# Expert outputs scattered with an add onto normalised rows in DRAM, instead of two stored rows per token

## The reference

```python
x = x + gnn(layernorm(x), edges, ...)
h = layernorm(x)                                    # "normalised rows"
# for every row: the 2 best of 16 experts, softmax weights w0, w1 over the two logits
moe = w0 * expert_e0(h) + w1 * expert_e1(h)         # expert: relu(h @ w1 + b1) @ w2 + b2, 256 -> 512 -> 256
y = h + moe
out = x + layernorm(y) * gamma + beta
```

## Time and profile before

| | |
|---|---|
| median of 3 runs | 1053.31 us (1049.52 to 1053.36) |
| the profiled execution | 1059.64 us |
| its span | 1057.8 us |
| engine busy in the span | PE 698.1, DVE 687.2, POOL 456.7, ACT 417.3 us |
| mean granted TensorE clock | 0.82 of 2.4 GHz |
| DMA | 178.11 MB, 168 GB/s over the span |

### The profile page before, as it was taken

One profiled execution on the slowest core, in us unless ns is written; L12 is line 12 of the kernel. 1 busy time (PEld: TensorE's weight loads), 2 busy tenths in 40 slices (PEclk: granted clock), 3 DMA queues, 4 the chain that ended last, 5 costly groups with the idle time before them and its releaser, 6 DMA issues. The chain is left out here.

```text
span 1057.8 us, 21646 instructions
## 1 busy us (share of the span) xinstructions
PE 698.1 (66%) x6132; PEld 609.6 (58%) x6132; DVE 687.2 (65%) x1486; ACT 417.3 (39%) x1089; POOL 456.7 (43%) x655
## 2 busy tenths in 40 slices
PE   3666878887515334230499999999999999970000
PEld 3553655555204333230399999999999999960000
DVE  7998999999269988812145555555444444435984
ACT  5933777776112222220133333333334333321331
POOL 9200000000002888845057777777555555540422
PEclk9997899999655555555599999999999999995555
DMA  9906756752171342224677766767676676625672
GB/s 290 247 7 49 191 160 159 174 173 52 57 237 51 116 143 98 84 74 141 242 210 216 211 212 212 214 211 212 213 214 211 212 211 213 211 81 174 243 240 70
DMA packets 100597, 178.11 MB, mean 168 GB/s; under 512 B 25247, under 2 KB 69153, under 8 KB 97055
## 3 DMA queue, kind: packets, MB, share of 16 engines
q1 hardware_dynamic: 75092, 145.28, 45.8%
q0 software_dynamic: 10512, 27.88, 7.5%
q10 hardware_dynamic: 14880, 3.60, 2.8%
HBM read 139.53 MB, written 37.20 MB: 167 GB/s over the span
## 5 line engine op out<-in xcount | busy, mean ns | idle before, releaser
L1133 PEld LDWEIGHTS PS<-W 128*128 128x128 f32 x1808 | 221.8, 193 | 8.7 <-issue 2.1
L1133 PE MATMUL PS<-W 128*128 128x128 f32 x1808 | 222.6, 277 | 2.2 <-DMA W<-in_L_ffn_w 1.7
L1144 PE MATMUL PS<-W 128*128 x904 | 213.7, 379 | 0.0
L1144 PEld LDWEIGHTS PS<-W 128*128 128x128 f32 x904 | 164.1, 191 | 17.5
L1291 POOL DMA_INDIRECT ys<-W x113 | 121.6, 1076 | 115.5 <-DVE W L1249 88.2
L691 DVE TENSOR_TENSOR W<-R,W 128x3584 bf16<-128x3584 bf16 (+1 forms) x104 | 159.4, 1590 | 0.0
L859 POOL DMA_INDIRECT xs<-W,slot_i x98 | 120.9, 1234 | 88.2 <-DVE slot_i L1008 59.9
L1221 DVE TENSOR_SCALAR W<-PS,b1T 128x128 f32<-128x128 f32 x226 | 70.2, 347 | 115.3 <-PE PS L1133 84.5
L1174 ACT ACTIVATE W<-PS 128x256 f32<-128x256 f32 x113 | 43.3, 383 | 257.3 <-PE PS L1121 155.2
L544 ACT ACTIVATE W<-PS 112x1024 f16<-112x1024 f32 x104 | 105.7, 1020 | 40.1 <-PE PS L603 38.7
L863 POOL MEMSET R<- 128x261 f32 x1 | 0.3, 317 | 254.3 <-POOLq L360 254.3
(11 more groups left out here) (215 smaller groups left out, 1154.5 us busy)
## 6 DMA issues: line engine op xcount, KB each, us to landing
W<-in_L_ffn_w SPq DMA_DIRECT2D x129, 512.0 KB, 8.8
W<-key_rows SPq DMA_DIRECT2D x26, 896.0 KB
W<-xs SPq DMA_DIRECT2D x113, 130.5 KB
W<-ys SPq DMA_DIRECT2D x6, 1792.0 KB, 8.1
XH<-in_x SPq DMA_DIRECT2D x6, 896.0 KB, 11.2
W<-in_x SPq DMA_DIRECT2D x7, 768.0 KB
out<-W SPq DMA_DIRECT2D x6, 896.0 KB, 4.1
W<-in_L_ffn_b ACTq DMA_DIRECT2D x1, 2048.0 KB, 7.5
```

The lines of the kernel that those rows point to most:

```text
L1133: last = nc.tensor.matmul(PS[:, 2 + 2 * u + j // 2, (j % 2) * P:(j % 2 + 1) * P], W1S[:, b, k, j * P:(j + 1) * P], XT3[:, u, k, :], start= ...
L1144: last = nc.tensor.matmul(PS[:, 6 + u, 0:C], HT3[:, u, j, :], wt2(e * W2COLS, j), start=(j == 0), stop=(j == 3))
```

## The change

`ys` now has one row per token, and behind them the rows for padding slots. The routing stage writes the normalised rows of each group there. The expert stage's scatters carry `compute_op=ALU.add`: the DMA reads the destination row, adds, and writes it back. Since two experts' tiles may meet in one row, `send(t)` waits until the scatter of tile t − 1 has landed. With the normalised row already in DRAM, ACT's `keep`, its buffer `Z1` and its semaphore go, `base_of` has one tensor input instead of two, and SP's reload of `X3[b]` waits for POOL's and ACT's small reads of that buffer in place of `keep`. The last stage reads one row per token (896 KB a group), DVE has no sum of two rows, and the residual is added by DVE where POOL did it.

```diff
-TRASH = 2 * NT * P
+TRASH = NT * P
...
+                def keep_rows(g, u, last):
+                    sp.wait_ge(xn_ready, GT * (g + 1))
+                    head = (GT - 1) * P
+                    sp.dma_start(ys[ds(g * (GT * P), head), :].rearrange("(t p) c -> p t c", p=P),
+                                 xn[:, u, 0:GT - 1, 0:C]).then_inc(xn_kept[u], 16)
+                    rows = LAST if last else P
+                    sp.dma_start(ys[ds(g * (GT * P) + head, rows), :], xn[0:rows, u, GT - 1, 0:C]).then_inc(xn_kept[u], 16)
+
+                def load_and_keep(g, i, u, last):
+                    load_x(g, i, u, last)
+                    if not (isinstance(g, int) and g == 0):
+                        keep_rows(g - 1, 1 - u, False)
+                pairs(sp, load_and_keep)
+                keep_rows(NGT - 1, 0, True)
...
                     wait_past(act, xn_sent[u], (16 * 2 * GT) * i)
+                    wait_past(act, xn_kept[u], 32 * i)
...
-                        sp.wait_ge(kept_ready, t + 1)
+                        sp.wait_ge(ratio_ready, t + 1)
+                        sp.wait_ge(first_ready, t + 1)
...
-                def keep(t):
-                    b = t % XBUFS
-                    act.wait_ge(first_ready, t + 1)
-                    if t >= 2:
-                        act.wait_ge(base_ready, t - 1)
-                    act.activation(Z1[:, t % 2, :], X3[:, b, 0:C], ACT.Copy, scale=first[:, b:b + 1]).then_inc(kept_ready, 1)
...
-                    nc.vector.scalar_tensor_tensor(Z3[:, t % 2, :], b2_bc[:, ds(e, 1), :].rearrange("p o c -> p (o c)"),
-                                                   weight[:, b:b + 1], Z1[:, t % 2, :], ALU.mult, ALU.add).then_inc(base_ready, 1)
+                    nc.vector.tensor_scalar(Z3[:, t % 2, :], b2_bc[:, ds(e, 1), :].rearrange("p o c -> p (o c)"),
+                                            weight[:, b:b + 1], None, ALU.mult).then_inc(base_ready, 1)
...
                 def send(t):
                     b, o = t % XBUFS, t % OBUFS
                     pool.wait_ge(o_ready, t + 1)
+                    if t >= 1:
+                        pool.wait_ge(o_sent[(t - 1) % OBUFS], 16 * ((t - 1) // OBUFS + 1))
                     nc.gpsimd.indirect_dma_start(
                         out=ys[:, :], out_offset=bass.IndirectOffsetOnAxis(ap=home[:, b:b + 1], axis=0),
-                        in_=O3[:, o, :], in_offset=None).then_inc(o_sent[o], 16)
+                        in_=O3[:, o, :], in_offset=None, compute_op=ALU.add).then_inc(o_sent[o], 16)
...
-                    y = y_two[u]
-                    nc.vector.tensor_tensor(y[:, :, 0, :], y[:, :, 0, :], y[:, :, 1, :], ALU.add).then_inc(y_summed, 1)
-                    dve.wait_ge(y_summed, g + 1)
                     for j in range(GT):
-                        ins = nc.vector.bn_stats(st4[:, j, :], y[:, j, 0, :])
+                        ins = nc.vector.bn_stats(st4[:, j, :], y_two[u][:, j, :])
...
+                    dve.wait_ge(scaled_ready, g + 1)
+                    nc.vector.tensor_tensor(scaled[u], scaled[u], XH[:, g * GT:(g + 1) * GT, :], ALU.add
+                                            ).then_inc(out_ready, 1)
...
-            @block.gpsimd
-            def _(pool):
-                for g in range(NGT):
-                    u = g % 2
-                    pool.wait_ge(scaled_ready, g + 1)
-                    nc.gpsimd.tensor_tensor(scaled[u], scaled[u], XH[:, g * GT:(g + 1) * GT, :], ALU.add
-                                            ).then_inc(out_ready, 1)
```

More of the change, by code:

```diff
@@ L180, in build @@
         O3 = take([OBUFS, C], fp32)
-        Z1 = take([2, C], fp32)
         Z3 = take([2, C], fp32)
@@ L193, in build @@
         take, at = carve(W, 0)
-        y_two = [take([GT, 2, C], fp32) for _ in range(2)]
+        y_two = [take([GT, C], fp32) for _ in range(2)]
         y_hat = [take([GT, C], fp32) for _ in range(2)]
@@ L386, in _ @@
                 const(pool.memset(cnt_in[:, :, :], 0.0))
-                const(pool.iota(tokc[:, :], pattern=[[2 * P, NT]], base=1, channel_multiplier=2,
+                const(pool.iota(tokc[:, :], pattern=[[P, NT]], base=0, channel_multiplier=1,
                                 allow_small_or_imprecise_dtypes=True))
@@ L807, in build @@
         token_set = sem("token_set")
+        xn_kept = [sem("xn_kept0"), sem("xn_kept1")]
         logits_sent = sem("logits_sent")
@@ L837, in load_x @@
                                  ).then_inc(xin_in[u], 16)
-                pairs(sp, load_x)
+                def keep_rows(g, u, last):
[11 more added lines that the diff above has]
+                keep_rows(NGT - 1, 0, True)
                 sp.wait_ge(pads_ready, 1)
@@ L849, in _ @@
                 sp.wait_ge(pads_in, 16 * (E + 1))
+                for u in range(2):
+                    sp.wait_ge(xn_kept[u], 32 * (NGT - NGT // 2 if u == 0 else NGT // 2))
             @block.gpsimd
@@ L1075, in build @@
         home_ready = sem("home_ready")
-        kept_ready = sem("kept_ready")
         base_ready = sem("base_ready")
@@ L1210, in _ @@
                         ratio_of(t + 1)
-                    keep(t)
             @block.vector
@@ L1274, in prepare @@
                     pool.wait_ge(first_ready, t + 1)
-                    nc.gpsimd.tensor_scalar(home[:, b:b + 1], X3[:, b, C + 4:C + 5], first[:, b:b + 1], trash[:, t:t + 1],
-                                            ALU.subtract, ALU.min
+                    nc.gpsimd.tensor_scalar(home[:, b:b + 1], X3[:, b, C + 4:C + 5], trash[:, t:t + 1], None, ALU.min
                                             ).then_inc(home_ready, 1)
@@ L1304, in build @@
         y_in = [sem("y_in0"), sem("y_in1")]
-        y_summed = sem("y_summed")
         st4_ready = sem("st4_ready")
@@ L1323, in load @@
                         sp.wait_ge(hat_ready, GT * (g - 1))
-                    sp.dma_start(y_two[u][:, 0:full].rearrange("p t k c -> p t (k c)"),
-                                 ys[2 * g * GT * P:2 * (g * GT + full) * P, :].rearrange("(t p k) c -> p t (k c)", p=P, k=2)
+                    sp.dma_start(y_two[u][:, 0:full], ys[g * GT * P:(g * GT + full) * P, :].rearrange("(t p) c -> p t c", p=P)
                                  ).then_inc(y_in[u], 16)
                     if g == NGT - 1:
-                        sp.dma_start(y_two[u][0:LAST, GT - 1].rearrange("p k c -> p (k c)"),
-                                     ys[2 * (NT - 1) * P:2 * N, :].rearrange("(p k) c -> p (k c)", k=2)
-                                     ).then_inc(y_in[u], 16)
+                        sp.dma_start(y_two[u][0:LAST, GT - 1], ys[(NT - 1) * P:N, :]).then_inc(y_in[u], 16)
                 def store(g):
@@ L1403, in hat @@
                     for j in range(GT):
-                        act.activation(y_hat[u][:, j, :], y_two[u][:, j, 0, :], ACT.Identity, bias=nm4[:, u, j:j + 1],
+                        act.activation(y_hat[u][:, j, :], y_two[u][:, j, :], ACT.Identity, bias=nm4[:, u, j:j + 1],
                                        scale=rs4[:, u, j:j + 1]).then_inc(hat_ready, 1)
```

1 line of the change is left out of this document (removed).

## The result

The changed kernel takes 1173.14 us (median of 4 runs, 1170.18 to 1174.14) against 1053.3 before: ratio 1.1155 (the two medians alone give 1.114), interval 1.1121 to 1.119, so 11 to 12% slower. The profiled execution took 1172.89 us, its span 1171.1.

What follows compares the result with a forecast made beforehand. PE was taken to bound the expert stage and a ring through POOL's addition the last stage. Last stage −28.2, expert loop 0, its end +2.8 and routing 0 sum to −25.4 us: 1053.31 to 1027.9, range 1022 to 1112.

Steps and rivals of the forecast that it cites:

- the scatters become the pace: Expert-stage rival: landings above 3.4 us lengthen the loop; 1120 us at a 4.2 us landing; chance 0.35.
- I take 3.2 us, and the loop costs 0: Expert stage: an accumulating scatter lands after 3.2 us, so waiting for it adds nothing to the 3.75 us tile.
- I take 0.35 with the semaphore: Expert stage: POOL needs 0.35 us from a scatter's landing to the next start, from 0.30 between back-to-back scatters.
- the limit for the landing: Expert stage: an accumulating scatter may take 3.4 us to land before the loop lengthens beyond 3.75 us.
- the bounds of 2.6 and 4.6: Accumulating scatter's landing: 2.6 us if the destination read hides entirely, 4.6 with a complete DRAM read ahead of the write.
- A plain scatter that waits for its predecessor would have a period of 2.95: Expert stage: a plain landing of 2.6 us plus 0.35 to the next start, against the tile's 3.75.
- Last stage, −28.2: Last stage: 28.2 us saved from 101.15, between −22 with slow loads and −31; groups 8.2 us apart.
- the two paths of the prediction: Last stage: ring through ACT at 8.2 us per group, or 7 us loads pacing two groups in 18.4 us.
- POOL's list has 0.2 us to spare with `beta`: Expert stage: POOL's own work plus 0.35 takes 3.55 us of 3.75 in the 49 tiles with `beta`.
- small overrun: Expert-stage rival: landing of 3.4 to 3.6 us or longer descriptors give back 5 to 22 us; chance 0.10.
- End of the stage, +2.8: End of the expert stage: the last scatter waits 3.55 us instead of 1.38 and lands 0.6 later, adding 2.8 us.
- Routing stage, 0: Routing stage: 14 added stores cost 0, with 0 to +13 us if ACT's cover were gone.

Runs made afterwards that it cites:

- b_wait: Kernel before, plain scatters, with only the wait for the previous scatter added: 1152.14 us, ratio 1.0843.
- b_wait_light: Kernel before plus the wait, plain scatters, half the first weights' bytes loaded from tile 4 on: 1103.04 us, ratio 1.0384.
- b_wait_noload: Kernel before plus the wait, plain scatters, no first weights loaded after tile 3: 1063.38 us, ratio 1.0024.
- t_nowait: Changed kernel with two rows per token, accumulating scatters without the wait, last stage reading one of the rows: 1043.47 us, ratio 0.9813.
- t_wait2: Changed kernel with two rows per token, accumulating scatters waiting for the one two tiles ago, last stage reading one row: 1046.51 us, ratio 0.9838.

## Why the prediction was wrong

The forecast was 1027.9 us, faster; measured is 1173.1, and outside the range. The side had been the first rival, "the scatters become the pace", with 0.35, and its case went further than its price of 1120. What failed is the step "I take 3.2 us, and the loop costs 0": the waiting scatters had a loop of 3.2 + 0.35 = 3.55 us in the sum, under PE's 3.75, and the runs show 5.07. Three things make up the difference of 1.5 us.

- **"I take 0.35 with the semaphore", from landing to the next start: 0.43 too little.** It is 0.78. The 0.30 came from a scatter that followed another on POOL. The same rows held another kind of release: the scatter at 705.22 started 0.76 us after DVE's L1249 had ended (703.98 + 0.48 = 704.46), and 0.76 is the median of that distance over all 113. With 0.78 the limit for the landing is 2.97 us instead of 3.4, already below the 3.2 that the sum went by.
- **"I take 3.2 us" for the accumulating scatter: 0.7 too little.** Alone it takes 3.9. The first byte moves 0.5 us later, and the movement takes 1.4 us where the sum had doubled 0.39 to 0.8. It was inside the bounds of 2.6 and 4.6, and the loop would have grown by this alone.
- **The landing was taken from its place in the old schedule: 0.4 too little.** Beside the loads the mean landing of the accumulating scatter is 4.28. For the plain one this is nearly all there is: "A plain scatter that waits for its predecessor would have a period of 2.95" became 4.52. The 2.6 was the landing of a scatter whose load came 1.3 us behind it. b_wait, b_wait_light and b_wait_noload show it.

Together 4.28 + 0.78 = 5.06, and 5.07 was measured. The rival had the right formula. With the measured 4.2 and its own 0.35 it gives a step of 4.55.

- The Trainium skill, DMA: Bandwidth & Descriptors, § Latency and other measured facts, was quoted with 0.2 us of HBM access on average and 2 us at high load. The measured 4.2 lies between the 3.2 and the 5.0 us that the two figures gave, and neither figure decided the case.
- **Last stage, −28.2: the size was right, at −27.2.** The first load took 5.14 us (5.2 forecast), the small instruction 0.18, and two groups are 16.3 us apart (16.4). But the path runs through the loads, which took 4.8 to 6.6 us where 4.1 had been taken from the store. At 5.15 a load is just at the point where the two paths of the prediction are equally long, so some of this was luck. From the chain of waits after:

```profile
1097.14 5.14 DMA W<-ys
...
1122.04 0.18 DVE W L1373
1122.21 0.02 issue
1122.24 3.56 ACT W L1408 x7
1125.81 5.15 DMA W<-ys
...
1138.33 0.18 DVE W L1373
```

- **POOL's list has 0.2 us to spare with `beta`: the size was wrong.** With the longer scatter POOL's list takes 4.02 us there in t_nowait, 0.27 more than PE. This is the "small overrun" of the rivals; the 9 tiles after `beta` made some of it up, and the stage grew by 10.7 us.
- **End of the stage, +2.8: not so.** The last start came 4.69 after the one before (1.38 before), but the gap behind it shrank by 1.8. That gap is 8.7 us in every run with accumulating scatters and 10.5 in every run with plain ones, however long the last landing was, so it does not follow the landing as the sum had it. The cause stays open.
- **Routing stage, 0: no cost is to be seen.** The stage's first scatter came 8.2 us earlier, not later. In the other runs it starts at 528.0 to 534.4 us with the stores and at 527.8 to 534.5 without them, so the 8.2 belongs to this profile, and its cause was not sought.

## What to carry to other kernels

Where each transfer waits for the one before, the pace is the landing plus the time from there to the next start. Take the second from a row with the same kind of release, not from back-to-back issues. A transfer's landing holds for its place in the schedule: ask what is issued within two microseconds on either side, and what it will meet if it starts late. And ask whether the other engines' lists, and the loads with them, move along when it is late, as they did here; then it stays late. Two in flight gave all of it back (1046.5 against 1187.3), but only with each scatter on rows of its own: on the change's shared rows two in flight could meet in one row.

## What the runs showed of the hardware

- POOL started a scatter 0.28 to 0.30 us after its own last instruction (t_nowait, before), 0.76 us after a release by DVE (before), and 0.75 to 0.80 us after the landing that it waited for (110 of 112 in after).
- A plain scatter of 128 rows of 1 KB landed after 2.5 us with no load near it, and after 4.5 to 4.7 us with a load of 512 KB issued within half a microsecond of its start (b_wait).
- An accumulating scatter of 128 rows of 1 KB was 144 packets against 48 for the plain one. Its bytes were under way for 1.4 us against 0.39, about 3.5 times as long. POOL's instruction took 1.63 us instead of 1.08, and the small one behind it 0.87 instead of 0.31. The Trainium skill, Collectives: The Full Stack, § The bandwidth ceiling: the fold count and why AG ≠ RS ≠ AR, says of ring collectives that a reduction runs at about half the rate of a copy, since the add reads two sources. This scatter is another kind of transfer, and lost more: moving took more than three times as long, and the packets had tripled.
- Beside 512 KB loads the accumulations cost no more than POOL's longer instruction when two or more could be in flight, at a DMA share of 0.86 (t_nowait, t_wait2).

Left open: whether a wait only at the change of expert, where rows can meet, would keep the correct sum with two scatters in flight. Tiles and experts are known only at run time, and it was not tried.
